# Attention and graph convolution on 16 samples: a new order with a place for each step of each sample

## What is computed

```python
x = x + linear_attention(gn32(x))       # q, k, v of 4 heads x 32
x = x + two_graph_convs(gn32(x))

# linear_attention(x): softmax of q over a head's 32 channels, of k over the tokens
context = einsum(k, v)                  # 32 x 32 for each head
out = w_out @ (context applied to q) + b_out
out = norm over the whole sample, times weight, plus bias

# two_graph_convs(x): tokens as rows, xf is 1024 x 64
xn  = xf / norm of each row
sim = xn @ xn.T                         # 1024 x 1024
val, idx = top_k(sim, 9);  v = val / (val.sum() + 1e-6)
out = sum over the 9 neighbours of v * (xn @ w1)[idx] + b1
out = silu(group_norm(out, 4 groups))
out = the same with w2, b2, and silu(group_norm(...)) again
```

## Time and profile before

| | |
|---|---|
| runs of the kernel | 685.97, 688.77, 689.89 us |
| median | 688.77 us |
| span of the profiled execution (the page gives no other time of it) | 685.7 us |
| median less span | 3.07 us |
| PE busy | 621.9 us, 91% |
| POOL busy | 499.2 us, 73% |
| DVE busy | 536.6 us, 78% |
| ACT busy | 449.2 us, 66% |
| chain that ended last | PE 33%, POOL 24%, issue 16%, DVE 10%, DMA 9%, ACT 7% |

### The profile page before, as it was taken

How to read it: one execution, slowest core, us unless ns; L and a number is a source line. 1 busy time by engine, 2 the same in 40 slices (tenths; PEclk the granted TensorE clock), 3 DMA queues, 4 the chain that set the end, 5 groups by cost and what they waited for, 6 DMA issues and landing times.

```text
span 685.7 us, 12336 instructions
## 1 busy us (share of the span) xinstructions
PE 621.9 (91%) x3824; PEld 310.4 (45%) x3824; DVE 536.6 (78%) x1008; ACT 449.2 (66%) x942; POOL 499.2 (73%) x534
## 2 busy tenths in 40 slices
PE   8878899898999999898999999999999999899874
PEld 6654535353444535353544435353535444333441
DVE  3357879788898889797888988898898988857821
ACT  2356477685868767784868768786868686743321
POOL 0224877788797978879797978788897979786810
PEclk9999999999999999999999999999999999979997
DMA  3002533434353535444363634445353534353411
GB/s 94 1 17 46 115 72 79 88 83 96 81 110 69 109 77 110 80 90 92 80 109 62 113 79 108 87 87 100 91 94 63 109 77 98 74 108 78 63 32 31
DMA packets 148722, 55.76 MB, mean 81 GB/s; under 512 B 138008, under 2 KB 138512, under 8 KB 148656
## 3 DMA queue, kind: packets, MB, share of 16 engines
q1 hardware_dynamic: 148656, 54.97, 39.6%
HBM read 12.87 MB, written 4.32 MB: 25 GB/s over the span
## 4 chain that ended last, share of the span: by engine, by line
PE 33%; POOL 24%; issue 16%; DVE 10%; DMA 9%; ACT 7%; SPq 1%; POOLq 0%; ACTq 0%; DVEq 0%
PE pC L974 18%; POOL adj L389 10%; PE pS L930 5%; POOL adj L384 5%; DMA rbc<-rn_row 4%; DMA rn_row<-rnT 4%; ACT adj L527 2%; PE pB L775 2%; DVE kstat L607 2%; ACT ek L458 2%; POOL res L407 2%; PE pA L814 2%; POOL qn L348 2%; POOL xn L372 2%; DVE top L683 2%
## 5 line engine op out<-in xcount | busy, mean ns | idle before, releaser
L974 PE MATMUL pC<-adj,xt 128*64 128x512 f32 x992 | 233.1, 603 | 2.9 <-POOL adj L395 1.6
L389 POOL TENSOR_TENSOR adj<-maskT,adj 128x128 f32<-128x128 f16 (+3 forms) x127 | 163.5, 1287 | 27.0 <-DMA maskT<-mask 25.2
L683 DVE MAX8 top<-pS 128x8 f32<-128x1024 f32 x128 | 155.6, 1224 | 33.1 <-ACT adj L527 32.9
L701 DVE MATCH_REPLACE8 mask<-top,pS 128x1024 uint16<-128x1024 f32 x128 | 155.2, 1213 | 0.0
L930 PE MATMUL pS<-xn 64*128 64x512 f32 x256 | 146.9, 661 | 7.3 <-issue 6.5
L930 PE MATMUL pS<-xn,xsw 64*128 64x512 f32 x256 | 146.2, 662 | 2.9 <-DVE mask L701 2.9
L527 ACT COPY adj<-pS 128x1024 f32<-128x1024 f32 x128 | 128.3, 1003 | 30.3 <-PE pS L932 30.2
L384 POOL TENSOR_TENSOR adj<-maskT,adj 128x128 f32<-128x128 f16 (+6 forms) x111 | 128.4, 1157 | 0.0
L974 PEld LDWEIGHTS pC<-adj,xt 128*64 128x64 f32 x992 | 64.0, 137 | 103.3 <-issue 94.7
L395 POOL TENSOR_TENSOR adj<-adj,selves 128x128 f32<-128x128 f32 x127 | 58.5, 461 | 8.7
L932 PEld LDWEIGHTS pS<-mark,place 64*128 64x128 f16 x256 | 24.7, 97 | 77.3 <-issue 77.3
(11 more groups left out here) (154 smaller groups left out, 1097.0 us busy)
## 6 DMA issues: line engine op xcount, KB each, us to landing
xs<-x SPq DMA_DIRECT2D x32, 128.0 KB, 2.8
vbc<-v_row SPq DMA_DIRECT2D x32, 128.0 KB, 2.9
rbc<-rn_row SPq DMA_DIRECT2D x30, 128.0 KB, 2.9
xsw<-xn SPq DMA_DIRECT2D x30, 128.0 KB, 2.3
out<-res SPq DMA_DIRECT2D x30, 128.0 KB, 2.3
maskT<-mask SPq DMA_TRANSPOSE x128, 3.1
cst<-packed SPq DMA_DIRECT2D x1, 471.5 KB, 3.6
y1sw<-y SPq DMA_DIRECT2D x2, 128.0 KB, 2.3
```

The costliest lines, as they stand in the source:

```text
L389: pool.tensor_tensor(above, m[:, r, 0:r + 1, :].bitcast(F16), above, ALU.mult).then_inc(done["upper"], 1)
L683: dve.max(top[b % 2][:, r, 0:TOP], pS[r % 2][:, :]).then_inc(done["tile_top"], 1)
L701: dve.match_replace(out=mask[n % MASKS][:, :], in_to_replace=top[b % 2][:, r, 0:TOP], in_values=pS[r % 2][:, :], imm_value=ONE_BITS).then_ ...
L974: mm = pe.matmul(ps[h * C:(h + 1) * C, 0:H], xt[:, t % NJ, t // NJ, :], adj[b % 2][:, t, h * H:(h + 1) * H], start=(t == 0), stop=(t == NT ...
```

## The change

**The table.** `BEGINS` and `TIMES` give way to `PLACES`: for every engine, stage, sample and step the place in that engine's list. So samples may differ in their pattern. `weave` sorts by these places. Where DVE's work on the last tile was called from `tops`, it is now a stage `late` with a place of its own.

**The begin.** DVE's ten copies become `constants()`, called behind the first sample's `qs`, with a semaphore `made` of their own. The weights' product becomes `products()`, into pC and behind the first average, and ACT copies `u` after it has read that average. The average and the keys of sample 1 move ahead of norms of sample 0.

**pB.** The waits written out by hand are replaced by `turn(use, b)`, which finds the use of pB that stands before this one in the order and waits until it has been read. `vT` now goes into pB and no longer into pC, also for the last sample. The first aggregation waits for `g2_read` of the sample before and no longer for the copy of `vT`.

**Fillers.** `WARM` has new numbers, and a bank for each.

```diff
-BEGINS = [0, 40.3551, 80.6227, 121.0734, 161.3839, 202.0138, 242.3515, 282.6959, 323.22, 363.5685, 404.1094, 444.49,
...
+PLACES = {
...
+        "unit": [
+            [10, 13, 15, 18], [27, 30, 34, 36], [50, 59, 65, 69], [93, 101, 107, 111], [135, 143, 149, 153],
...
-    ("start", 0): 36, ("k", 0): 20, ("ekT", 0): 9, ("qT", 0): 9, ("att", 0): 7, ("at_mean", 0): 16, ("in_mean", 1): 6,
-    ("mi_mean", 0): 32, ("k", 1): 9, ("ss", 0): 8, ("att", 1): 6, ("sim1", 0): 2, ("mi_mean", 1): 24, ("k", 2): 9,
-    ("xt1", 1): 24, ("g1_mean", 14): 18, ("sim7", 15): 12, ("g2_mean", 14): 18, ("g1_mean", 15): 12, ("xt2", 15): 21,
-    ("a2_0", 15): 5, ("ky", 0): 18,
+    ("start", 0): (36, "pC"), ("k", 0): (23, "pA"), ("ekT", 0): (7, "pC"), ("ky", 0): (14, "pB"), ("qT", 0): (7, "pC"),
+    ("att", 0): (9, "pB"), ("k", 1): (12, "pA"), ("mi", 0): (14, "pB"), ("ss", 0): (14, "pB"), ("att", 1): (9, "pB"),
+    ("in", 2): (5, "pB"), ("mi", 1): (9, "pB"), ("ss", 1): (5, "pB"), ("rnT", 1): (8, "pB"), ("m", 2): (11, "pC"),
+    ("sim0", 1): (14, "pS0"), ("att", 2): (9, "pB"), ("g2", 13): (8, "pB"), ("g1", 14): (5, "pB"),
+    ("xt2", 14): (14, "pC"), ("a2", 14): (5, "spare"), ("xt2", 15): (14, "pC"), ("a2", 15): (5, "spare"),
+    ("g2", 15): (14, "pB"),
...
+EMPTIED = {"in": "in_veps", "yT": "yT_copied", "ky": "ky_copied", "m": "m_copied", "att": "att_copied", "at": "at_veps",
+           "mi": "mi_veps", "ss": "ss_read", "xt1": "xt1_copied", "vT": "vT_copied", "g1": "g1_veps", "g2": "g2_veps"}
...
+        def turn(use, b):
+
+            place = PB_TURNS.index((use, b))
+            return emptied(*PB_TURNS[place - 1]) if place else (done["prepared"], PREPARED)
...
-                    live += [(BEGINS[b] + at, steps) for at in TIMES[engine][stage.__name__]]
+                    next(steps, None)
+                    live += [(at, steps) for at in PLACES[engine][stage.__name__][b]]
...
-            act.wait_ge(done["u_ps"], 1)
-            act.copy(u[:, :, :], pB[:, 0:HEADS * C].rearrange("c (h o) -> c h o", h=HEADS)).then_inc(done["u_ready"], 1)
...
                 deviation(b, "in", pB)
+                if b == 0:
+                    act.wait_ge(done["u_ps"], 1)
+                    act.copy(u[:, :, :], pC[:, 0:HEADS * C].rearrange("c (h o) -> c h o", h=HEADS)).then_inc(done["u_ready"], 1)
...
+                if b < 1:
+                    constants()
...
-                if b < B - 1:
-                    copy_weights(b, pC[0:NT, 0:P])
+                copy_weights(b, pB[0:NT, 2 * P:3 * P])
...
                 average(b, "in", pB, "avg_pair")
-                yield
+                if b == 0:
+                    products()
...
+                pe.wait_ge(*turn("vT", b))
+                warm("vT", b)
+                pe.wait_ge(*of("v_rec", b))
+                pe.transpose(pB[0:NT, 2 * P:3 * P], vrec[b % 2][:, :], ident).then_inc(done["v_T"], 1)
```

More of the change, by code:

```diff
@@ L755, in convolve @@
                         dve.tensor_tensor(res[b % 2][:, cols], y3[:, cols], x1[b % XBUFS][:, cols], ALU.add).then_inc(done["late_res"], 1)
-            weave("vector", attend, unit, tops, masks, convolve)
+            weave("vector", attend, unit, tops, masks, late, convolve)
         @block.tensor
@@ L761, in _ @@
             pe.wait_ge(done["prepared"], 1)
-            for _ in range(WARM[("start", 0)]):
+            for _ in range(WARM[("start", 0)][0]):
                 pe.matmul(pC[:, 0:2 * P], still[:, 0:P], still[:, :], start=True, stop=True)
@@ L765, in _, with products @@
             pe.wait_ge(done["prepared"], PREPARED)
-            for h in range(HEADS):
-                for c in (slice(0, C), slice(C, P)):
-                    mm = pe.matmul(pB[c, h * C:(h + 1) * C], wvo[:, 0, h, :], wvo[:, 1, h, :], start=True, stop=True)
-            mm.then_inc(done["u_ps"], 1)
-            pe.wait_ge(done["u_ready"], 1)
+            def products():
+                for h in range(HEADS):
+                    for c in (slice(0, C), slice(C, P)):
+                        mm = pe.matmul(pC[c, h * C:(h + 1) * C], wvo[:, 0, h, :], wvo[:, 1, h, :], start=True, stop=True)
+                mm.then_inc(done["u_ps"], 1)
             def average(b, tag, ps, avg):
                 n = channels[tag]
+                pe.wait_ge(*turn(tag, b))
+                warm(tag, b)
                 pe.wait_ge(*of(f"{tag}_spread", b))
@@ L852, in attend @@
                 pe.wait_ge(*of("ky_copied", b))
[L853 removed]
+                if b == 0:
+                    pe.wait_ge(done["u_ready"], 1)
+                pe.wait_ge(*turn("m", b))
                 for h in range(HEADS):
@@ L864, in attend @@
                 yield
+                pe.wait_ge(*turn("att", b))
                 warm("att", b)
```

216 lines of the change are left out of this document (90 added, 126 removed), and 144 rows, old and new, of the table PLACES.

## The result

The changed kernel takes 669.72 us (median of 4 runs, 668.66 to 674.62), the kernel before in the same runs 687.37 (684.38 to 689.89): a ratio of 0.9748, 95% interval 0.9698 to 0.9798. On the 688.77 us shown before that is 671.4; I had said 673.8, between 665 and 684. The profiled execution of the change is its longest, 674.62 us with a span of 672.8; the other three have spans of 666.9 to 668.8. So its trace holds 4 to 6 us that the other executions don't have.

A forecast was written before the change was run, and what follows sets the result against it. TensorE, busy 91% of the span, was taken as the bound, with 63.8 us idle. Terms −6.0 − 8.2 + 4.1 − 6.9 + 2.0 = −15.0 us took the span from 685.7 to 670.7, forecasting 673.8 us, range 665 to 684.

The forecast's parts named there:

- Start, −6.0: Up to the first aggregate: earlier statistics, reordered norms and fewer fillers bring it to near 88.3, −6.0 us (bounds 0 and −8).
- the larger one: Hand-over to sample 1: its norm, keys and queries move ahead, so the first similarity comes at about 44.2, −4.1 us.
- the step at the first norm: Begin: with the constant copies moved behind, first statistics come 1.34 us sooner, of which the first key product sees 1.05.
- Middle, −8.2 and +4.1: Middle samples: GpSimd's new order removes the waits for qn and the diagonal, −8.2 us; vT in pB costs +4.1 us.
- The wait for `qn`: Middle, TensorE waiting on GpSimd: qn ahead of lower removes this wait, −6.6 us of the −8.2.
- The other step, +4.1: Middle: the at average waits for Vector's row copy behind a MAX8, 0.31 us in 13 samples (bounds 0 and 8.2).
- Tail, −6.9 and +2.0: Last samples: sample 15's first aggregation starts 6.9 us sooner; idle time without fillers slows the clock, +2.0 us.
- The 2.0 us for the clock: Tail: about 2.5 us idle before the average slows xt2 and 16 aggregates, 0.95 + 1.04 us (lower bound 0).
- The first: Rival, middle: the at average waits for a whole MAX8, 1.9 us in 13 samples, slower at 694.4 us; chance 0.06.
- The second: Rival, start: gains nothing because the first aggregate waits for its adjacency from GpSimd, 679.8 us; chance 0.14.
- The third: Rival, tail: idle time drops the clock to 1.2 GHz for xt2 and the whole last aggregation, 679.8 us; chance 0.10.
- The fourth: Rival, middle: qn waits reappear at the next wait, as rnT's way over three DMAs sets the period, 677.9 us; chance 0.10.

The follow-up runs named there:

- the run again: The changed kernel run once more with nothing different, against the kernel before: 670.11 us, ratio 0.9777.
- xs_ahead: Changed kernel with SP's loads of xs for samples 7 to 15 put back right ahead of the rn_row store: 674.33 us, ratio 0.9820 to the kernel before.
- pool_old: Changed kernel with GpSimd's order in the middle samples as before the change: 670.95 us, ratio 0.9798 to the kernel before.
- tail_fill: Changed kernel with 16 fillers in TensorE's idle gap behind sample 15's first aggregation: 671.75 us, ratio 0.9787 to the kernel before.
- xs_moved: Changed kernel with the last two xs loads right ahead of rn_row (samples 7 and 15) moved later: 670.97 us, ratio 0.9771 to the kernel before.
- table_early: Changed kernel with one added two-column ScalarE copy at its very begin: 669.06 us, ratio 0.9745 to the kernel before.
- constants_first: Changed kernel with Vector's ten constant copies ahead of the first statistics again: 677.00 us, ratio 0.9847 to the kernel before.

## Why the prediction was right, and where it was not

In all, −15.0 us were forecast, and by the ratio it is −17.4. The parts came out as follows.

**Start, −6.0.** Right in its sum: −5.9 in the run again (98.66 against 104.60), −2.7 in the profiled execution, which had one late transfer, and −7.0 in two other kernels with the same start. Of its two parts only the first, the constants, was run back; that the larger one comes from the new order in the hand-over rests on the timelines alone. Inside, the step at the first norm was mis-sized. I took the first statistics from 7.49 to 6.15, where Vector's first constant began. That start was itself the wait for the constants; `x` had landed by 4.30. So −3.2 us, not −1.34. But the constants are needed by the spread and the average too, and the average gained only 1.92 (7.04 against 8.96) and the first `kstat` 1.47, where I had carried 1.05. The rest of the sum came out as priced, with the first aggregate at 88.42 in the run again; where one transfer was late, the clock fell at `xt1`, and it was 91.68.

**Middle, −8.2 and +4.1.** The sum of −4.1 was near (−5.4 and −7.0 measured), and both steps under it were wrong, so that it came near is luck. The wait for `qn` did go, and GpSimd's new order is enough for that (xs_ahead), but its going shortened no period: with the load of `xs` ahead again a period has a median of 37.6 us, as before, and with the old order on GpSimd back but the load away it stays at 36.9. I had read a wait by its releaser and looked at what stood ahead of that on the same engine. What counted for the period was what stood ahead of the whole chain, on SP: a load ahead of the 4 KB store on which `rbc`, `xn` and the next similarity depend. The term took the total of a wait, 6.6 us, as if the periods would be shorter by all of it, and left out the similarity ahead of it, while what the order on SP gives is 0.5 us a sample. SP's order, which the change alters too, is not in the term. The other step, +4.1, priced 0.31 us in 13 samples; it was 0.37 in 3 samples, 1.1 us. Undone, with Vector's order as it is but for the copy, it makes the kernel slower by 4.3 us in the median, so there is nothing to get back by it: I had costed the new place of `vT` against the old order of Vector, not against the new.

**Tail, −6.9 and +2.0.** −4.8 in all against −4.9 forecast, again with two errors that cancel. The first aggregation of 15 starts 88.65 us after the last `kstat` in place of 93.60, −4.95 and not −6.9: the second aggregation of 14 gained 1.9 us and not 2.9, and TensorE waits 0.91 us for the diagonal. The 2.0 us for the clock are 0.1 (32.49 us from there to the end, against 32.35). Its rows were misread. In the trace of before the clock had fallen 4 us ahead of that `xt2`, and ahead of its gap of 1.65 us, as this pass of a similarity shows, which takes 0.69 us elsewhere:

```profile
599.57 1.16 PE L930 MATMUL pS<-xn,xsw 64*128 64x512 f32 x1 [0.78 <-DVE mask L701]
```

So the 0.95 and 1.04 us are not what that gap did. And in the change a slow clock between average and `xt2` costs next to nothing, since `xt2` waits there for ScalarE's `y`: it starts 3.58 us behind the average where the 14 fillers took 2.98 us, and 3.35 behind it in the run again, where they took 1.70. The Trainium skill (TensorE: Matmul & The Clock Gate, "Part 1: The HAM clock gate") says that the clock is throttled by default and that activity releases it. The profiled execution agrees: it fell over 2.16 us of idle time, and the fillers behind it took the slow stretch on themselves, so that `xt2` ran in 1.16 us. But the run again shows that such a gap need not cost anything, with 2.69 and 1.44 us of idle time and no slow instruction behind them, so the rule gave no size here.

**The rivals.** The first didn't happen but has its mechanism shown: 1.2 us at the copy cost 21 us. The second happened in part and for another reason: 3.3 us between the first similarity and the first aggregate are lost in some executions (`rbc` came 2.8 to 3.0 us after `rn_row` in the profiles of the change, pool_old, tail_fill and xs_moved), to a late `rn_row` and not to GpSimd. The third did not happen. The fourth, that a period is set by the way from `rnT` over the DMAs to the next similarity, was the nearest to the truth of the middle, and I gave it 0.10: xs_ahead shows the period following that way, with the wait for `qn` gone and the wait at the similarity in its place. Only its time was wrong, since the change made the way shorter.

## What to carry to other kernels

When a wait goes away, look first whether the period got shorter with it, since the lost time can be met at another wait of the same chain. Then ask for the first step of the chain that came sooner, by laying one period of both traces over each other from a common start; the releaser of the wait, and what stands ahead of it on its engine, is only the last link. A large transfer that nobody waits for should not stand right ahead of a small store that everybody waits for. And a table of places is one piece: taking one step of it back to where it stood can cost more than the step was ever priced at, because the others were placed around it.

## What the runs showed of the hardware

The time from the store of a 4 KB row (`rn_row`) to the issue of the DMAs that wait for it is mostly 1.20 to 1.25 us where no load of `xs` was issued just ahead of it. With a load of 256 KB just ahead it is mostly 1.8 to 2.3 us (1.45 to 3.49 over 43 cases in all runs). Without such a load it was over 1.25 us in 35 of 153 cases, up to 3.19, and no run shows why. (The last store of each run, behind which other things stand, is left out.)

In the profiled execution of the change two idle gaps of TensorE in the middle, 1.51 us for `rn` behind a late transpose of a mask and 1.75 us for `xsw`, went with periods of 39.66 and 40.44 us at a granted clock of 0.96, 2.8 and 3.5 us over a regular one: about half of that is not the wait but the slow clock behind it. The length of a gap alone doesn't decide, and neither does its place: ahead of the last average but one, 2.16 us of idle time were followed by fillers at half clock in the profiled execution and 2.69 us by fillers at full clock in the run again, which is the same kernel. A gap of 1.55 us in the tail of before cost nothing behind it.

An activation table load of 1.28 us ran at 0.73, long before what its instruction waited for, in the kernel before and in table_early, where it belonged to a copy at the head of ScalarE's program. In the change and in constants_first, where it belongs to the first spread, it ran only when the aggregate that the spread waits for had ended (5.30 and 8.63).
